# Splitting the query features' row tops before the turn, with one selector product in place of two

## The reference

```python
xp = jnp.einsum('bhnd,md->bhnm', x * norm, proj)            # 16 heads, 64 features
diag = jnp.sum(jnp.square(x), axis=-1, keepdims=True) * 0.5 * (norm * norm)
stab = jnp.max(xp, axis=-1, keepdims=True)                  # is_query: one top per token and head
return ratio * (jnp.exp(xp - diag - stab) + EPS_K)
```

## Time and profile before

| | |
|---|---|
| timed runs, us | 794.2, 793.9, 793.23 (median 793.9) |
| span of the profiled execution, us | 792.5 |
| TensorE products busy | 731.3 (92%), 6012 records |
| TensorE weight loads busy | 597.2 (75%) |
| VectorE busy | 618.3 (78%) |
| ScalarE busy | 470.0 (59%) |
| GpSimd busy | 372.2 (47%) |
| mean granted TensorE clock | 0.965 of full speed |

### The profile page before, as it was taken

One profiled execution on the slowest core, in us unless ns is written; L12 is line 12 of the kernel. 1 busy time (PEld: TensorE's weight loads), 2 busy tenths in 40 slices (PEclk: granted clock), 3 DMA queues, 4 the chain that ended last, 5 costly groups with the idle time before them and its releaser, 6 DMA issues. The chain is left out here.

```text
span 792.5 us, 16189 instructions
## 1 busy us (share of the span) xinstructions
PE 731.3 (92%) x6012; PEld 597.2 (75%) x6012; DVE 618.3 (78%) x1298; ACT 470.0 (59%) x749; POOL 372.2 (47%) x358
## 2 busy tenths in 40 slices
PE   8999999999999999999999979985899999999950
PEld 7867768778778778778778658875788889998850
DVE  5877678888888888788788696888858777777683
ACT  4656747767867867857857734464145544455470
POOL 4364407517517517517617512501337666445663
PEclk9999999999999999999999999989699999999985
DMA  8100010011011011011011011150256664556593
GB/s 249 33 2 2 1 54 2 27 54 56 28 54 54 26 53 54 26 53 54 26 53 30 28 57 52 57 194 0 70 178 168 159 153 99 122 152 167 117 276 118
DMA packets 51184, 62.60 MB, mean 79 GB/s; under 512 B 9408, under 2 KB 44992, under 8 KB 51136
## 3 DMA queue, kind: packets, MB, share of 16 engines
q1 hardware_dynamic: 44016, 49.74, 19.3%
q0 software_dynamic: 6864, 12.19, 8.0%
q10 hardware_dynamic: 256, 0.03, 0.0%
HBM read 40.85 MB, written 21.10 MB: 78 GB/s over the span
## 5 line engine op out<-in xcount | busy, mean ns | idle before, releaser
L2157 PE MATMUL pF<-w,h 128*128 128x256 f32 x448 | 109.8, 386 | 0.0
L2157 PEld LDWEIGHTS pF<-w,h 128*128 128x128 f32 x448 | 80.7, 190 | 17.6 <-issue 8.6
L1128 POOL DMA_INDIRECT kp<-row_scratch,idx_g x32 | 42.4, 1325 | 76.7 <-DVE idx_g L1829 52.8
L893 ACT ACTIVATE h<-pX,b1cur 128x512 f32<-128x512 f32 x64 | 44.1, 691 | 55.9 <-DVE b1cur L1929 41.5
L982 POOL TENSOR_SCALAR ve<-mv 128x4 f32<-128x4 f32 x36 | 8.5, 237 | 141.4 <-DVE mv L1205 140.5
L2607 PE MATMUL pX<-w_lo,h_hi 128*128 128x256 f32 x256 | 73.9, 289 | 0.8 <-issue 0.8
L2607 PE MATMUL pX<-w_hi,h_lo 128*128 128x256 f32 x256 | 72.4, 283 | 0.0
L2607 PE MATMUL pX<-w_hi,h_hi 128*128 128x256 f32 x256 | 72.4, 283 | 0.0
L1136 POOL DMA_INDIRECT acc_scratch<-qp,idx_s x28 | 56.6, 2021 | 21.7 <-DVE qp L1866 16.8
L1887 DVE TENSOR_TENSOR h_lo<-h,h_hi 128x512 fp32r<-128x512 f32 x64 | 42.8, 690 | 25.9 <-ACT h_hi L885 25.9
L1305 DVE RECIPROCAL den<-den 128x512 f32<-128x512 f32 x14 | 46.9, 3348 | 7.4 <-ACT den L541 7.4
(11 more groups left out here) (434 smaller groups left out, 2171.9 us busy)
## 6 DMA issues: line engine op xcount, KB each, us to landing
kp<-fc1T SPq DMA_DIRECT2D x8, 1024.0 KB, 7.1
w<-fc2T SPq DMA_DIRECT2D x8, 1024.0 KB, 8.1
xin<-video SPq DMA_DIRECT2D x7, 512.0 KB, 3.8
x<-video SPq DMA_DIRECT2D x7, 512.0 KB, 4.5
out<-x SPq DMA_DIRECT2D x7, 512.0 KB, 3.0
acc_scratch<-xf SPq DMA_DIRECT2D x7, 512.0 KB, 2.9
row_scratch<-y SPq DMA_DIRECT2D x7, 512.0 KB, 3.0
kp<-acc_scratch SPq DMA_DIRECT2D x4, 512.0 KB, 5.7
```

What stands on the lines that cost most here:

```text
L893: nc.scalar.activation(h[:, n, :], pM[n % M_SLOTS], ACT.Gelu_apprx_tanh, bias=b1cur[:, n:n + 1]).then_inc(he_ready, 1)
L1128: pool.indirect_dma_start(xg[:, g, :], None, row_d, bass.IndirectOffsetOnAxis(ap=idx_g[:, g:g + 1], axis=0)).then_inc(gathered, 16)
L2157: ins = nc.tensor.matmul(pF[m][:, half * D:(half + 1) * D], h[:, k, tok(2 * m + half)], w2[:, k, :], start=(k == 0), stop=(k == FC - 1))
```

## The change

The tops are written to a buffer of their own, `mxq` (64 columns). While they still lie in token order, two small operations on VectorE, `parts_of_tops`, write into `mxp` their high part (rounded to fp32r) and the rest, in columns 0 to 3 and 4 to 7 of each group of 32. One turn brings both, and ScalarE's copy is `mxT`. The selector's entries are now set for both sets of rows, so that one product adds high and low part. `rest_of_tops`, `mxT_lo` and the second tops product are gone. `parts_of_tops` stands between `q_max` 3 and `k_sub` 2 on VectorE, and `turn_tops` waits for it. On TensorE, two of the eight products of `ff_out(0, 1)` (four records) are moved ahead of `turn_tops`. In the preparation there is one reduction more.

```diff
+TOPS = TT + 2
...
-        mxT_hi, mxT_lo = sb("mxT_hi", [P, N], F32R), sb("mxT_lo", [P, N], F32R)
+        mxT = sb("mxT", [P, N], F32R)
...
-                wait(act, ql_ready, i * 2)
+                wait(act, ql_ready, i)
...
-                nc.scalar.activation(mxT_hi[:], pXall[:, 0, :], ACT.Copy).then_inc(mxT_ready, 1)
+                nc.scalar.activation(mxT[:], pXall[:, 0, :], ACT.Copy).then_inc(mxT_ready, 1)
...
-            def rest_of_tops(i):
-
-                dve.wait_ge(mxT_ready, i + 1)
-                nc.vector.tensor_tensor(mxT_lo[:], pXall[:, 0, :], mxT_hi[:].bitcast(F32), ALU.subtract).then_inc(ql_ready, 1)
...
-                nc.vector.tensor_reduce(mxp[:, t, :].rearrange("p (a r) -> p a r", a=4)[:, :, 0:4],
+                nc.vector.tensor_reduce(mxq[:, t, :].rearrange("p (a r) -> p a r", a=4),
...
+            def parts_of_tops(i):
+
+                dve.wait_ge(qmx_ready, i * TOPS + TT)
+                wait(dve, x_ready, 0 if is_first(i) else (i - 1) * X_JOBS + J_MT + 1)
+                whole = mxq[:].rearrange("p t (a r) -> p (t a) r", r=4)
+                hi, lo = (mxp.rearrange("p t (a k r) -> p (t a) k r", a=4, r=4)[:, :, k] for k in range(2))
+                nc.vector.tensor_copy(hi.bitcast(F32R), whole).then_inc(qmx_ready, 1)
+                dve.wait_ge(qmx_ready, i * TOPS + TT + 1)
+                nc.vector.tensor_tensor(lo, whole, hi, ALU.subtract).then_inc(qmx_ready, 1)
...
                     q_max(i, 3)
+                    parts_of_tops(i)
                     k_sub(i, 2)
                     k_sub(i, 3)
-                    rest_of_tops(i)
...
-            built.link(nc.vector.tensor_reduce(of_head[:], ident[:].rearrange("p (a r) -> p r a", a=4)[:, 0:4], AX_X, ALU.add))
+            built.link(nc.vector.tensor_reduce(of_rows[:], ident[:].rearrange("p (a r) -> p r a", a=4)[:, 0:8], AX_X, ALU.add))
+            built.link(nc.vector.tensor_reduce(of_head[:], of_rows[:].rearrange("p (k r) -> p r k", k=2), AX_X, ALU.add))
...
-                    pe.wait_ge(ql_ready, (i + 1) * 2)
+                    pe.wait_ge(mxT_ready, i + 1)
...
                     slot_x(i, J_MT)
+                    pe.wait_ge(qmx_ready, (i + 1) * TOPS)
...
-                             (selm[:, g].rearrange("p k m -> p (k m)"), mxT_hi[:]), (selm[:, g].rearrange("p k m -> p (k m)"), mxT_lo[:]))
+                             (selm[:, g].rearrange("p k m -> p (k m)"), mxT[:]))
...
                     ff_out(0, 0)
+                    ff_out(0, 1, 0, 2)
                 if att:
                     turn_tops()
                 if ff:
-                    ff_out(0, 1)
+                    ff_out(0, 1, 2, FC)
```

More of the change, by code:

```diff
@@ L166, in build @@
         of_16 = sb("of_16", [P, 8])
+        of_rows = sb("of_rows", [P, 8])
         of_head = sb("of_head", [P, 4])
@@ L172, in build @@
         mxk = sb("mxk", [P, TT, H])
+        mxq = sb("mxq", [P, TT, H])
         kmax = sb("kmax", [P, H])
@@ L1385, in first_batch @@
                 q_max(0, 3)
+                parts_of_tops(0)
                 k_sub(0, 2)
-                rest_of_tops(0)
                 k_sub(0, 3)
@@ L2056, in slot_x @@
                 elif n <= J_MT:
-                    pe.wait_ge(qmx_ready, i * TT + 2 * (n - J_XQ))
+                    pe.wait_ge(qmx_ready, i * TOPS + 2 * (n - J_XQ))
                 elif n == J_QT:
-                    pe.wait_ge(ql_ready, (i + 1) * 2)
+                    pe.wait_ge(mxT_ready, i + 1)
                 else:
@@ L2190, in features_turned @@
                     if g == 0:
-                        pe.wait_ge(qsq_ready, (i + 1) * 2)
+                        pe.wait_ge(ql_ready, i + 1)
                     parts = ((projbd[:], qT[:, g, :]), (selc[:].rearrange("p k m -> p (k m)"), qsq_hi[:, g, :]),
                              (selc[:].rearrange("p k m -> p (k m)"), qsq_lo[:, g, :]),
-                             (selm[:, g].rearrange("p k m -> p (k m)"), mxT_hi[:]), (selm[:, g].rearrange("p k m -> p (k m)"), mxT_lo[:]))
+                             (selm[:, g].rearrange("p k m -> p (k m)"), mxT[:]))
                     for n, (w_, x_) in enumerate(parts):
```

## The result

The changed kernel takes 789.1 us (median of 4 runs, 787.51 to 791.14) against 793.76 before (4 runs, 793.23 to 794.2). The ratio is 0.9941 with a 95% interval of 0.9924 to 0.9958: 4.7 us less (the interval allows 3.3 to 6.0), where 4.2 were forecast, and faster by more than what a measurement can tell. The profiled execution took 789.41 us with a span of 787.7; before, the span was 792.5. What lies around the span is 1.7 here, where the forecast had set 1.4.

A forecast was written before the change was run, and what follows sets the result against it. TensorE was taken to bound the attention batches. Batches 1 to 7 gain 0.57 us each (4.0), with batch 0 4.2: span 792.5 to 788.3, plus 1.4 around it 789.7 us; range 788.4 to 791.9.

The forecast's parts named there:

- TensorE sets these batches, and a set costs the distance of its starts: Attention batches: each `features_turned` loses one set of four row-tiled products, 0.23 us each, 0.46 a batch.
- A real stall of 0.15 at the turn, which the moved records remove: `turn_tops` in batches 1 to 7 waits 0.15 us for VectorE's last reduction; removing this gains 1.05 us.
- The pair costs 0.54: VectorE's two new 128x64 operations ahead of `turn_tops` take 0.54 us with their waits (0.45 to 0.68).
- What could hold the second group's products: `features_turned(1)` needs `exp_q(0)` out of PSUM; it fits with 0.02 us to spare, limiting a batch's gain to there to 0.4.
- three signs that the prediction named: Prediction wrong if the pair exceeds 0.7 us, `features_turned(1)` waits for `exp_q(0)`, or the low clock stretches grow.
- The rest of a batch moves along: Work behind `exp_q(1)` moves with it; GpSimd's sums of keys don't move, end at 215.78, wanted at 216.5: not late.
- Batches 1 to 7: 4.0 forecast: Each gains 0.46 + 0.15 = 0.61 us, less 0.04 for two tight places: 0.57 x 7 = 4.0.
- Batch 0: net gain of 0.2 forecast: Fillers behind the later turn start the first products 0.24 us later; sets gain 0.46: net 0.2 (0 to 0.5).
- the clock variant of rival B: A longer wait ahead of batch 0's turn keeps the low clock over 4.2 us worth of full-speed work: 793.9 us.
- Rival A: ScalarE or the pair takes part of the gain: 1.6 to 3.4 us gained, 790.5 or 791.9 us; chance 0.22.
- Rival B: No change: the removed products are hidden, or something later takes back the 1.8 us won anyway; chance 0.08.
- Rival C: The pair's copy waits 1.05 us for GpSimd, the turn comes late and the kernel gets slower, 796.6 us; chance 0.04.

The follow-up runs named there:

- experiment 1: The kernel before without the selector product on the low parts of the tops, which are then missing in the sum; 789.89 us against 793.63.
- experiment 3: The kernel before with only the four records of `ff_out(0, 1)` moved ahead of `turn_tops`; 792.32 us against 793.63.
- experiment 2: The kernel after with the four `ff_out` records put back behind the turn; 793.8 us against 793.63 for the kernel before.
- experiment 5: The kernel after with ScalarE's two denominator copies ahead of the last of four `xf_norm` tiles; 788.1 us against 793.77 for the kernel before.
- experiment 8: The kernel after with VectorE's residual behind the next batch's statistics instead of right behind `k_sub`; 788.63 us against 793.77 for the kernel before.
- experiment 7: The kernel after with both earlier denominator copies and 3 instead of 5 fillers behind batch 0's turn; 788.97 us against 793.77 for the kernel before.
- experiment 4: The kernel after with one more GpSimd addition beside VectorE's pair in batches 1 to 7, result overwritten; 804.13 us in one run.
- experiment 6: The kernel after with 3 instead of 5 filler products behind batch 0's turn; 787.97 us against 793.77 for the kernel before.

## Why the prediction was right, step by step

*TensorE sets these batches, and a set costs the distance of its starts.* Right: 0.46 a batch forecast, 0.48 by experiment 1, and 3.7 us in the timed runs (793.63 - 789.89).

*A real stall of 0.15 at the turn, which the moved records remove.* Right, and a little small: experiment 3 gives 0.16 to 0.24 a batch. The 0.15 was read in batch 3 and taken for seven, but in batches 1, 2 and 7 the stall was 0.22; the 2.6 us of the earlier trace rows over seven waits, 0.37 each against the 0.34 of batch 3, already said so. That the pair needs this cover, and that without it the stall would be 0.69, was confirmed by experiment 2 with 0.71.

*The pair costs 0.54.* It took 0.58 from the reduction's end: 0.195 and 0.224, and 0.16 for waits, where 0.10 was set. The row of the same shape was a good guide, though that operation has an input in PSUM and the pair has none.

*What could hold the second group's products.* These start at 212.56, ScalarE's `exp_q(0)` ends at 210.64 + 1.86 = 212.50. Their weight load is now put down to it:

```profile
212.56 0.31 PEld L2208 LDWEIGHTS pX<-qT,projbd 32*128 32x128 f32 x8 [0.20 <-ACT qp L624]
```

By its words, that `features_turned(1)` waits for `exp_q(0)`, this is one of the three signs that the prediction named for being wrong. It costs nothing that can be seen: from the first group's products to the second's it is 212.56 - 208.29 = 4.27 us, in experiment 2, where TensorE is late and the same 0.20 is put down to issue, 213.88 - 209.59 = 4.29, and before 4.51, one set more. The limit was met within hundredths, as worked out.

*The rest of a batch moves along.* Here the prediction was incomplete. I had checked that GpSimd's sums of keys, which don't move with TensorE, come in time for `sums_of_keys`, and stopped there. What GpSimd does behind them, `nf` for `xf_norm`, is as immobile, and its first sum even became longer. ScalarE now waits 0.81 us for `nf`, and its denominators are late by 0.13. It took 0.1 us from each loop batch (experiment 5), and it was the pair's own doing (experiment 8). The allowance of 0.04 a batch for tight places was made for other places, and happened to be of that order.

*Batches 1 to 7: 4.0 forecast, 4.40 measured.* Batches 1 and 2 gave 0.70 and 0.75 against 0.55 to 0.66 in the others: both had the larger stall of 0.22, and neither had lost the tenth for `nf` (53.42 and 57.30 us long, and 53.43 and 57.31 in experiment 5). So two errors offset each other here, a stall that was set too small and a loss that was not seen.

*Batch 0: net gain of 0.2 forecast, 0.35 lost in the profile.* The mechanism ahead of the clock was right, the fillers decide (experiment 7). But the profiled execution had the low clock for longer. The granted clock by windows, kernel before and kernel after (TensorE busy, clock, DMA):

```profile
33.00:36.00 3.00, 2.58 (x13) 0.54 0.34 121
36.00:40.00 4.00, 3.70 (x34) 0.92 0.00 0
```

```profile
30.00:33.00 3.00, 2.98 (x22) 0.87 0.34 103
33.00:36.00 3.00, 2.58 (x13) 0.50 0.22 75
36.00:40.00 4.00, 4.00 (x26) 0.62 0.00 0
```

With 1.2 GHz as half of 2.4, that makes about 3.4 us at the low level before (2 x 0.46 x 3 + 2 x 0.08 x 4) and 6.8 after. This looks like the clock variant of rival B, but it isn't the change: by the same reckoning experiments 1 and 4 have 3.4 us, experiments 3, 6 and 8 have 6.8, and experiments 2, 5 and 7 none at all. Experiment 3 has no pair and still 6.8. So growing low stretches, the third sign that the prediction named, were no sign of anything: they come and go by themselves. Comparing traces with the same 3.4, the kernel before reaches the mark of batch 0 at 49.10 and experiment 4, whose batch 0 is that of the kernel after, at 48.68, 0.4 earlier. With 6.8, experiment 3, whose batch 0 is that of the kernel before, has 50.35, the kernel after 49.45 and experiment 8 49.15, 0.9 and 1.2 earlier. Single traces scatter here by tenths (experiment 1 has 48.93 with one product less than the kernel before), so a gain in batch 0 is likely, and its size is not shown. The profile's batch 0 was bad luck, and the 0.75 won in the rest of the program, where the low stretches also fell otherwise, was good luck; they nearly cancel in the 4.8. That the timed runs come so near the forecast (4.7 against 4.2) is luck as well, with an interval that reaches from 3.3 to 6.0.

*Rival A* is out for its own places, though something of its kind (ScalarE late in the second half) took a tenth. *Rival B* is out. *Rival C* did not occur because GpSimd idles where the pair stands, and experiment 4 shows that it would have, had GpSimd been at work there.

*Two slips in the sums.* A gain of 5.5 from 793.9 ends at 788.4, not 788.6. And the 1.4 around the span set a profile beside the median of other executions: in every recorded run the time lies 1.7 or 1.8 above its own span, which would have given 790.0 and not 789.7.

## What to carry to other kernels

A new wait on a saturated engine's path is free only under work that was put ahead of it: here four records made the difference between 4.7 us and nothing, since the product that was saved and the stall that its preparation caused weigh about the same. When one engine gets faster, follow those that don't move with it to the end of their list, not to their first consumer. A small copy between SBUF tiles on VectorE is cheap only where GpSimd is idle; look at GpSimd's row before placing it, and look at what it pushes into GpSimd's way behind it. Where two operations of these engines change in length together, compare their ends before their lengths: the ends showed a wait where the lengths had looked like a slowdown.

## What the runs showed of the hardware

- A one-input copy of 128x64 on VectorE waited for the end of a GpSimd addition: 1.42 us instead of 0.195, ending 0.05 behind it. A one-input operation of 16x16 did the same, 0.22 us alone and 0.90 to 1.27 beside an addition, always ending 0.02 to 0.03 behind it. The trace shows a wait for the whole operation. The Trainium skill's page "GPSIMD Engine Reference" (Key points) names contention of GpSimd with VectorE's operations in a two-port mode or with two inputs in SBUF.
- Two-input operations of 128x1024 on both engines wait for each other, each for the end of the one that started first, and don't share. The residual took 1.23 us alone and 2.80, 3.39 and 1.56 in three placements, always ending 1.08 or 1.09 behind GpSimd's first sum; that sum took 2.78 and 3.34 and always ended 2.21 to 2.24 behind `k_sub`.
- Not every operation of VectorE waits. Wholly inside a GpSimd addition in the kernel before, the reduction of 128x1024 out of PSUM took 1.21 to 1.23 us as elsewhere, and `rest_of_tops`, with one of its two inputs in PSUM, 0.68 (0.69 in batch 0, with GpSimd idle).
- The time at the low clock around 32 to 39 us came out as 0, 3.4 or 6.8 us in ten profiles of kernels that differ little up to there. The time of an unchanged kernel spreads as well: 25 runs of the kernel before went from 791.81 to 797.08 with mean granted clocks of 0.963 to 0.973, the shorter times mostly at the higher clock.
